# The last head group of an attention-and-FFN kernel: softmax sums spread by a 0/1 product instead of through SyncE transfers, and its rows moved from two queues

## What is computed

```python
xn = layernorm(x)
q, k, v = xn @ Wq, xn @ Wk, xn @ Wv            # 16 query heads of 16, 8 key/value heads
scores = einsum('bhqd,bhkd->bhqk', q, k) / sqrt(16) + where(mask, 0, -10000)
s = einsum('bhqk,bhkd->bhqd', softmax(scores), v) -> [B, S, 256] @ Wo
g = silu(gelu(xn @ w1q.T + b1) @ w2q.T + b2)    # ternary w1q, w2q
out = x + s * g
```

## Time and profile before

| | |
|---|---|
| median of 3 runs | 668.54 us (666.46 to 669.02) |
| the profiled execution | 668.7 us, span 666.9 us |
| PE busy | 565.5 us (85%) |
| ACT busy | 447.1 us (67%) |
| DVE busy | 405.1 us (61%) |
| POOL busy | 263.7 us (40%) |
| mean granted clock of TensorE | 0.946 of 2.4 GHz |

### The profile page before, as it was taken

The page is one execution under the profiler, slowest core; times in us unless marked ns, Lnnn a source line. Parts: engine busy times, 40 slices in busy tenths (PEclk is TensorE's granted clock), DMA queues, the critical chain, the costliest instruction groups (busy, mean ns, idle before and its releaser), DMA issues. The chain is left out here.

```text
span 666.9 us, 10897 instructions
## 1 busy us (share of the span) xinstructions
PE 565.5 (85%) x3725; PEld 291.2 (44%) x3725; DVE 405.1 (61%) x915; ACT 447.1 (67%) x576; POOL 263.7 (40%) x303
## 2 busy tenths in 40 slices
PE   0758499999999789998999699999899899899942
PEld 0657145343435355343445255443445365224412
DVE  5889567877476377877375377968385444411211
ACT  4335767876786557876777457876777667987740
POOL 3424633334426333333426243343436343444341
PEclk9879689999999789999999789999999799999987
DMA  8002442121322343011322333011322333011001
GB/s 244 0 1 69 119 120 71 32 61 25 98 60 61 120 97 90 25 57 27 97 61 57 98 110 96 27 56 34 94 63 54 82 116 91 24 55 49 23 11 51
DMA packets 51239, 45.45 MB, mean 68 GB/s; under 512 B 9072, under 2 KB 45552, under 8 KB 51184
## 3 DMA queue, kind: packets, MB, share of 16 engines
q1 hardware_dynamic: 50096, 43.95, 23.8%
q10 hardware_dynamic: 1088, 0.79, 0.4%
HBM read 11.41 MB, written 4.19 MB: 23 GB/s over the span
## 5 line engine op out<-in xcount | busy, mean ns | idle before, releaser
L1610 ACT ACTIVATE f_probs<-sc_ps,shift 128x1024 f32<-128x1024 f32 (+3 forms) x384 | 332.7, 901 | 109.1 <-PE sc_ps L1508 103.7
L1508 PE MATMUL sc_ps<-f_q_stack,f_k_stack 104*128 104x512 bf16 (+3 forms) x768 | 195.9, 345 | 34.0 <-ACT f_probs L1610 18.1
L1525 PE MATMUL att_ps<-f_probs,f_v_sb 128*32 128x512 f32 (+3 forms) x1536 | 168.4, 513 | 6.2 <-POOL f_probs L1668 6.2
L1661 POOL TENSOR_SCALAR_AFFINE_SELECT f_probs<-f_probs 128x512 f32<-128x512 f32 x128 | 94.3, 737 | 138.1 <-ACT f_probs L1610 137.0
L1508 PEld LDWEIGHTS sc_ps<-f_q_stack,f_k_stack 104*128 104x128 bf16 x768 | 48.3, 99 | 198.9 <-ACT f_probs L1610 124.2
L1668 POOL TENSOR_TENSOR f_probs<-f_probs,f_near 128x512 f32<-128x512 f32 x64 | 77.9, 1218 | 133.5 <-ACT f_probs L1610 133.5
L1449 PE MATMUL aux_ps<-w2T,f_h_hi 128*128 128x256 f32 x256 | 71.8, 314 | 0.0
L1648 POOL TENSOR_TENSOR f_h_lo<-f_hid,f_h_hi 128x512 fp32r<-128x512 f32 x36 | 47.2, 1320 | 43.8 <-DVE f_h_hi L1721 43.8
L1449 PE MATMUL aux_ps<-w2T,f_h_lo 128*128 128x256 f32 x256 | 62.7, 278 | 0.0
L1525 PEld LDWEIGHTS att_ps<-f_probs,f_v_sb 128*32 128x32 f32 x1536 | 31.3, 109 | 68.9 <-issue 44.3
L1711 DVE TENSOR_TENSOR f_probs<-f_probs,f_near 128x512 f32<-128x512 f32 x48 | 36.4, 758 | 32.8 <-ACT f_probs L1610 31.8
(11 more groups left out here) (198 smaller groups left out, 721.0 us busy)
## 6 DMA issues: line engine op xcount, KB each, us to landing
f_q_stack<-f_q_parts SPq DMA_DIRECT2D x192, 64.0 KB
f_k_stack<-f_k_parts SPq DMA_DIRECT2D x96, 64.0 KB, 2.2
xn<-in_L_attn_hidden_states SPq DMA_DIRECT2D x4, 1024.0 KB, 6.7
f_attT<-f_att_raw SPq DMA_DIRECT2D x128, 32.0 KB
f_rden_bc<-f_den SPq DMA_DIRECT2D x64, 64.0 KB
s_w_nat<-in_L_ffn_w SPq DMA_DIRECT2D x2, 1024.0 KB, 9.4
f_x_res<-in_L_attn_hidden_states SPq DMA_DIRECT2D x4, 512.0 KB, 4.4
out_y<-f_x_res SPq DMA_DIRECT2D x4, 512.0 KB, 3.2
```

The source lines that it names most:

```text
L1508: last = pe.matmul(sc_ps[:, 2 * u + hh, lo:CH], k_stack[0:KROWS + T, h // REP, kb * P:(kb + 1) * P], q_stack[0:KROWS + T, SLOT[n], 2 * u + ...
L1525: last = pe.matmul(att_ps[32 * q:32 * q + 32, n % 2, lo:CH], v_sb[:, kb, j * VW:j * VW + 32], probs[:, i % NPROB, q, lo:CH], start=(kb == ...
L1610: act.activation(probs[:, i % NPROB, us, lo:CH], sc_ps[:, us, lo:CH], ACT.Exp, bias=shift[:, 0:1], scale=HD ** -0.5).then_inc(exp_done, 1)
L1661: pool.affine_select(out=block_probs, in_=block_probs, compare_op=ALU.is_ge, fill=0.0, base=0, pattern=[[0, NQ], [1, P]], channel_multipli ...
```

## The change

A constant tile `pick` is filled in the first turn: two 128x128 matrices of 0 and 1. Matrix a has a 1 where the input row is the row of sums of a head of the last two groups (a = 0 for group 6, a = 1 for group 7) and the output row is one of that head's 16 rows in `attT`. In the last turn two new jobs on PE multiply `att_raw` of group 6 and of group 7 with them and add both up in one bank of `aux_ps`, so that all 128 rows hold their head's sums. DVE takes the reciprocal of that bank into `rden_bc[:, 1]` and multiplies `attT[:, 1]` with it. The last entry of `norms`, and with it the last `reciprocals`, `spread_rden` and `normalise_heads`, is gone; so is group 7's transfer to `den`. Group 7's four row transfers are issued by SP (two) and ACT (two). The copy of group 7 to `att_raw` also waits for the first of the new products.

```diff
+                pick = tile("pick", [P, 2, P])
...
                     if main and not prep:
+                        jobs += [(GROUP_END[6] + BEHIND + 2, "pick", 0), (NSTEP + 4, "pick", 1)]
                         jobs += [(NSTEP + 5, "out_proj", TC + t, n_prev + TC + t) for t in range(TC)]
...
                     if not prep:
-                        norms += [(NG - H // NQ // 2, (0,)), (NG, (1,))]
+                        norms += [(NG - H // NQ // 2, (0,))]
...
-                        if j[1] == "ffn_down" and j[3]:
+                        if j[1] == "ffn_down" and j[3] or j[1] == "pick" and j[2]:
                             bank_of.append(bank_of[-1])
...
                                 h = g * NQ
-                                for q in range(NQ):
+                                last_group = not prep and n == NG - 1
+                                for q in range(2 if last_group else NQ):
                                     row = (h % HT + q) * HD
                                     sp.dma_start(attT[row:row + HD, h // HT, :], att_raw[32 * q:32 * q + HD, :]).then_inc(att_in, 16)
-                                sp.dma_start(den[h * TC:(h + NQ) * TC, :], att_raw[HD:P:32, :]).then_inc(att_in, 16)
+                                if not last_group:
+                                    sp.dma_start(den[h * TC:(h + NQ) * TC, :], att_raw[HD:P:32, :]).then_inc(att_in, 16)
...
-                                    spread_rden(own + 2)
                                     for t in range(TC, T, 2):
...
+                                elif kind == "pick":
+
+                                    pe.wait_ge(att_out, NG - 1 + a[0])
+                                    last = pe.matmul(ps, pick[:, a[0], :], att_raw[:, :], start=(a[0] == 0), stop=(a[0] == 1))
...
+                                if not prep:
+
+                                    act.wait_ge(att_out, NG)
+                                    for q in range(2, NQ):
+                                        row = ((H - NQ) % HT + q) * HD
+                                        act.dma_start(attT[row:row + HD, QT - 1, :], att_raw[32 * q:32 * q + HD, :]).then_inc(att_in, 16)
...
+                                lk(pool.memset(pick[:, :, :], 0.0))
+                                for a in range(2):
+
+                                    lk(pool.affine_select(out=pick[:, a, :].rearrange("p (h d) -> p h d", d=HD), in_=pick[:, a, :].rearrange("p (h d) -> p h d", d=HD),
+                                                          compare_op=ALU.not_equal, fill=1.0, base=P * a - HD, pattern=[[-32, HT], [0, HD]], channel_multiplier=1))
...
+                                elif kind == "pick" and a[0]:
+                                    dve.wait_ge(aux_done, n + 1)
+                                    lk(dve.reciprocal(rden_bc[:, 1, :], ps))
+                                    dve.sem_inc(aux_free[bank], 1)
+                                    dve.wait_ge(att_in, 16 * ((NQ + 1) * NG - 1))
+                                    dve.tensor_tensor(attT[:, 1, :], attT[:, 1, :], rden_bc[:, 1, :], ALU.mult).then_inc(attT_done, 1)
...
                                 dve.wait_ge(pv_done, GROUP_END[n] + 1)
+                                if not prep and n == NG - 1:
+                                    dve.wait_ge(aux_done, 1 + [i for i, j in enumerate(jobs) if j[1] == "pick"][0])
...
                                 for j in jobs_at(NSTEP + BEHIND - 0.5, 999):
-                                    if j[1] == "out_proj" and j[2] == TC:
-                                        reciprocals(own + 2)
-                                        normalise_heads(own + 2)
                                     job(*j)
```

More of the change, by code:

```diff
@@ L1432, in job @@
                                 ps = bank_ps(bank)
-                                if before_it and not (kind == "ffn_down" and a[1]):
+                                if before_it and not (kind == "ffn_down" and a[1] or kind == "pick" and a[0]):
                                     pe.wait_ge(aux_free[bank], before_it)
```

## The result

The changed kernel takes 664.13 us (median of 17 runs) against 668.88 of before in the same runs: ratio 0.9927, 95% interval 0.9913 to 0.9941, that is 3.9 to 5.8 us less. The profiled execution of it is the shortest of the 17: 661.63 us, with a span of 660.0. That is 7.1 us less than the profiled execution of before, and more than the change: its last copy ends at 641.36 of the span and not at 643.87, after work that is the same in both but for the first product and the filling of `pick`. In the profiled executions of all kernels of this document that copy ended anywhere from 641.4 to 646.6.

The account below looks back on a forecast made before the run. Latencies at the end, with no engine busy, were taken as the bound: 1.07 + 3.31 + 0.70 + 0.14 = 5.22 us replace 10.15, so 668.7 - 4.9 = 663.8 us; range 662.0 to 665.8.

Parts of the forecast that it names:

- What bounds the end: From group 7's copy to PE's restart: latencies set the time, 10.15 us all on the path, 5.22 in their place.
- Second product: Group 7's product with `pick` on PE after the last copy: 1.07 us at full clock.
- Reciprocal: DVE's 128x512 reciprocal from PSUM after the second product: 3.31 us, upper end 3.77; PSUM as source costs nothing.
- Handovers: Four handovers between engines in the new end chain, 0.02 to 0.04 us each, in all 0.14.
- First product: Group 6's product with `pick`, in PE's 1.15 us wait for ACT: needs 1.07 us, hidden, costs nothing.
- POOL at the start: One memset and two selections filling `pick`: 1.2 us with links, covered by POOL's idle 12.41 us, costs nothing.
- Second queue: Group 7's rows issued by SP and ACT: land about 646.9, 1.4 us to spare before the reciprocal's end, cost nothing.
- Projection: Output projection at the end, 14 PE instructions: half the clock again after 3.6 us idle, same 4.74 us.
- the clock that holds: Rival at the final projection: full clock makes it 1.1 to 1.8 us shorter, 662.0 to 662.7 us; chance 0.12.
- Late transfers: Rival at group 7's rows: ACT's transfers need up to 7.0 us to land, time 666.8 us; chance 0.09.
- an uncovered product: Rival at group 6's product: PE's next scores wait for it, up to 1.07 us back, 664.9; chance 0.06.
- the slower case: Rival at the 128x512 reciprocal: at 25.4 ns per element it takes 13.0 us, kernel 673.5 us; chance 0.02.

Follow-up runs that it names:

- tile by tile: Changed kernel with reciprocal and multiplication in four pieces of 128 columns, one per projection tile, sums in a bank of their own: 665.11 us, ratio 0.9941.
- the kernel that keeps PE busy: Changed kernel with seven more copies of the first tile's k = 0 product on PE during the reciprocal, results overwritten: 662.81 us, ratio 0.9892.
- the four kernels with a longer list: Changed kernel with reciprocal doubled (670.12 us), split in four pieces (665.11), cut to 128x32 (663.37), or one never-executed DVE instruction added (667.23).
- The version that had its list cut back: Changed kernel with 128x32 reciprocal, repeated products keeping PE busy, and DVE's list no longer than the changed kernel's: 659.92 us, ratio 0.9863.
- the kernel with the small reciprocal alone: Changed kernel with PE turning the sums, DVE inverting only 128x32, PE turning them back, instead of the 0/1 product: 663.37 us, ratio 0.9906.

## Why the prediction was right

Forecast 663.8, measured 664.13. By its steps:

- *What bounds the end.* 10.15 us were taken to be path from end to end, and 5.22 to take their place; 5.47 did. That the reciprocal has no slack is shown by doing it twice (3.40 us more).
- *Second product.* 1.07 forecast, 1.14 measured, at full clock.
- *Reciprocal.* 3.31 forecast from two sizes, 3.36 measured, so (3.36 - 0.942) / 384 = 6.3 ns per element beyond the first 128. PSUM as the source cost nothing that shows: 128 elements from it took 0.96 us (tile by tile), against 0.942. The Trainium skill ("VectorE: DVE Perf Modes", First, the fixed hardware budget) states a repeat count of 8 for the reciprocal; read as eight cycles per element at that page's clock it makes an estimate of 4.27 us. The 3.36 us do not bear that reading out.
- *Handovers.* 0.14 forecast, 0.27 measured: behind the reciprocal stand 0.03 + 0.02 + 0.09 us on DVE instead of one handover; there DVE's list waits for its own result and marks the bank free.
- *First product.* At nothing, as forecast: 7.63 and 7.64 us from the scores to the copy.
- *POOL at the start.* At nothing, as forecast: the filling of `pick` took 0.31 + 0.82 us, and POOL's idle time after it is still 11.07 us, 12.41 before.
- *Second queue.* At nothing, as forecast: 5.47 us with it and without. The landing was put at 1.4 us ahead of the reciprocal's end. With the reciprocal cut short it shows, as a multiplication that starts 2.96 us after the copy; the long reciprocal ends 4.6 us after it.
- *Projection.* That the clock would be at half again was right; that the projection would run as before was not. PE restarted at full clock, the fall came about a us later and the return towards the end of the projection. By the windows the slow part was some 0.5 us longer than before, so the length was 4.99 and not 4.74; that the two came so near is in part luck. The row of 236.57 had shown such a late fall, in windows that the prediction does not list:

```profile
236.00:237.00 1.00, 0.43 (x2) 0.41 (x3) 0.82 (x2) 0.00 (x0) 0.39 (x1) 1.00 1.11 172
237.00:238.00 1.00, 1.00 (x5) 0.80 (x4) 0.82 (x4) 0.00 (x0) 1.00 (x3) 0.56 1.07 321
```

So the eight instructions from 236.57 on did not all run at half the clock, and 2.9 us was too short a price for 14 at the full one: they take 3.29.

In sum 4.93 us were forecast; 10.15 - 5.47 and 4.74 - 4.99 make 4.4 within the profiles, and the runs say 3.9 to 5.8. That 663.8 lies only 0.3 us from the median is closer than the terms were, 0.25 us too low for the path and 0.25 for the projection: luck. Of the rivals, the clock that holds did not come true by itself; its price, 1.1 to 1.8 us, was confirmed by the kernel that keeps PE busy: 1.7 us, or 1.45 from the 4.74 that the forecast took. Late transfers and an uncovered product did not occur, and the slower case would have needed a reciprocal of 8.2 us.

## What to carry to other kernels

At a program's end, where no engine is busy, count latencies: nine issues one after another, with two landings to wait for, cost nearly twice what a product and a long reciprocal cost that need no transfer (10.15 and 5.47 us). After such a change the new longest step is to be sought at once; here it was the length of the reciprocal, which turning the sums to 32 columns cut from 3.36 to 0.36 us, and only then did the second queue begin to pay. If PE has to wait ahead of its last work, giving it products to repeat can be worth more than another us saved in the wait; here it was worth 1.7 us.

## What the hardware showed that I had not expected

One DVE instruction more than in the changed kernel, executed or not, made every execution exceed its span by 2 to 3 us more. The rest is 2.95 to 4.8 us in the four kernels with a longer list (medians 3.8 to 4.4) and 1.6 to 2.5 in all the others. The version that had its list cut back did not show it. So one instruction more is enough; whether the length of the list counts, or the place where it ends, is not shown. The Trainium skill ("Runtime: NRT & Kernel Launch", Instruction fetch mechanics) says that instructions are fetched in blocks and that a branch out of the fetched ones waits for a transfer. A program's end that moves into another block would look like this. The traces agree in part: in three of the four kernels one to four loads of instructions start more than 2 us after the span's end, and in none of the others; but the kernel with the small reciprocal alone has no such load either, with a rest of 4.25 us. So no run here shows whether that is the cause.

Issuing from two queues at the same time did not always cost the same. With the old path, SP's second issue took 0.88 us with ACT beside it; in the changed kernel it took 0.59 with ACT beside it, as alone, while ACT's second took 0.80 where its first took 0.59. So a general price for it is not shown.
